# Layer 2's normalizing, turning and first choice moved into the last turns of layer 1

## The reference, cut to what matters

```python
for layer in (0, 1, 2, 3):
    xn = _layernorm(x, axis=-1)
    x = x + attn[layer](xn) + ffn[layer](xn)
```

```python
logits = xt @ Wr + br
probs = jax.nn.softmax(logits, axis=-1)
gate, idx = jnp.max(probs, axis=-1), jnp.argmax(probs, axis=-1)
```

## Time and profile before

| what | value |
|---|---|
| median of three runs | 1791.4 us |
| lowest and highest | 1785.49 and 1794.98 us |
| the profiled execution | 1796.15 us |
| its span, first to last instruction | 1794.3 us |
| busy share of the span: PE, DVE, ACT, POOL | 84%, 64%, 48%, 25% |
| mean granted clock of PE | 0.915 |
| the chain that ended last: PE, DVE, issue, DMA, ACT, POOL | 59%, 15%, 9%, 5%, 4%, 4% |

### The profile page before, as it was taken

The page is one execution under the profiler, slowest core; times in us unless marked ns, Lnnn a source line. Parts: engine busy times, 40 slices in busy tenths (PEclk is TensorE's granted clock), DMA queues, the critical chain, the costliest instruction groups (busy, mean ns, idle before and its releaser), DMA issues.

```text
span 1794.3 us, 41191 instructions
## 1 busy us (share of the span) xinstructions
PE 1502.5 (84%) x11707; PEld 945.8 (53%) x11707; DVE 1149.0 (64%) x3266; ACT 866.6 (48%) x1971; POOL 445.7 (25%) x542
## 2 busy tenths in 40 slices
PE   5356899999998877999997478899999699999998
PEld 4112566656565355888886134455554245555554
DVE  6733566667566865666665556566667667777774
ACT  1022344444444423444442045566665268788887
POOL 3465223223222112222223521122222211000000
PEclk9996799999898858999996589999999779999999
DMA  8431344544543403233320223444442011111110
GB/s 261 127 136 58 102 152 136 175 123 148 160 129 101 116 1 130 107 141 141 129 107 21 97 65 114 135 138 138 138 138 76 21 42 52 53 50 52 47 51 12
DMA packets 127876, 184.77 MB, mean 103 GB/s; under 512 B 14657, under 2 KB 107217, under 8 KB 125345
## 3 DMA queue, kind: packets, MB, share of 16 engines
q1 hardware_dynamic: 94864, 144.54, 25.1%
q10 hardware_dynamic: 26112, 25.17, 4.8%
q0 software_dynamic: 6816, 14.02, 2.2%
HBM read 148.44 MB, written 42.84 MB: 107 GB/s over the span
## 4 chain that ended last, share of the span: by engine, by line
PE 59%; DVE 15%; issue 9%; DMA 5%; ACT 4%; POOL 4%; another core or an unknown queue 1%; SPq 1%; DVEq 1%; ACTq 0%; POOLq 0%
PE pH L528 8%; PE pO L733 7%; PE pT_ L594 6%; PE pY L541 6%; PE pH L620 6%; PE pY L628 5%; DVE mx L1339 3%; PE pS L676 3%; PE pS L698 3%; DMA stk<-packed_qk 2%; ACT pex L847 2%; PE pT_ L592 2%; POOL sorted_x L991 2%; PE pT_ L512 2%; DMA packed_qk<-qk 1%
## 5 line engine op out<-in xcount | busy, mean ns | idle before, releaser
L847 ACT ACTIVATE pex<-pT_ 128x512 f32<-128x512 f32 (+1 forms) x768 | 427.1, 560 | 495.8 <-PE pT_ L594 361.1
L1339 DVE TENSOR_REDUCE mx<-pS 128x2 f32<-128x512 f32 x512 | 347.9, 689 | 154.5 <-PE pS L571 107.5
L594 PE MATMUL pT_<-stk 32*128 32x256 f16 x1024 | 203.9, 285 | 90.9 <-DMA stk<-packed_qk 31.0
L888 POOL DMA_INDIRECT home_y<-ysb,home x117 | 115.1, 984 | 543.4 <-DVE ysb L1362 283.2
L571 PE MATMUL pS<-stk 32*128 32x256 f16 x1024 | 208.3, 291 | 27.6 <-DVEq L1082 17.6
L733 PE MATMUL pO<-pex,va 128*9 128x256 f32 (+1 forms) x3072 | 206.6, 390 | 2.6 <-ACT pex L847 2.6
L594 PEld LDWEIGHTS pT_<-stk 32*128 32x128 f16 x1024 | 55.7, 93 | 209.5 <-issue 86.4
L840 ACT ACTIVATE wb<-pH,b 128x256 f32<-128x256 f32 x256 | 107.3, 470 | 106.6 <-PE pH L528 106.2
L528 PE MATMUL pH<-XT,w 128*128 (+1 forms) x512 | 132.0, 386 | 1.1
L620 PE MATMUL pH<-xsT,wb 128*128 128x128 f32 x888 | 132.4, 294 | 0.3 <-ACT xsT L816 0.3
L851 ACT ACTIVATE pT_<-later 128x384 f32<-128x384 f32 x256 | 126.6, 494 | 8.1
(11 more groups left out here) (220 smaller groups left out, 2584.6 us busy)
## 6 DMA issues: line engine op xcount, KB each, us to landing
wb<-in_w SPq DMA_DIRECT2D x72, 514.0 KB
stk<-packed_qk ACTq DMA_DIRECT2D x96, 256.0 KB, 2.7
wb<-in_w SPq DMA_DIRECT2D x39, 578.0 KB
packed_qk<-qk SPq DMA_DIRECT2D x144, 128.0 KB, 2.0
wb<-gates_turned SPq DMA_DIRECT2D x8, 2048.0 KB, 7.0
pex<-gates_turned SPq DMA_DIRECT2D x8, 2048.0 KB, 7.1
xsb<-sorted_x SPq DMA_DIRECT2D x111, 64.5 KB, 4.1
sorted_x<-in_c_places SPq DMA_DIRECT2D x4, 1548.0 KB, 15.7
```

What stands on the lines that cost most here:

```text
L594: return pe.matmul(bank[:, part * T:(part + 1) * T], key, stk[rows, side, j, 0:T], start=True, stop=True)
L847: ins = act.activation(pex[:, k % 8, 0:n], bank[:, 0:n], ACT.Exp)
L888: pool.indirect_dma_start(YH, bass.IndirectOffsetOnAxis(ap=home[:, place_:place_ + 1], axis=0), ysb[:, place_, :], None).then_inc(sem(f"ho ...
L1339: ins = dve.tensor_reduce(mx[:, :, j, col], bank.rearrange("p (c n) -> p c n", c=2), AX.X, ALU.max)
```

## The change

Seven of layer 2's eight groups leave its prologue. Turn 10 + g of layer 1 now handles group g (tiles 4g to 4g + 3, rows 2g and 2g + 1), for g from 0 to 6: all their rows have been final for some turns. `q` is POOL's inverse deviation (DVE first signals that the statistics are there), `x` DVE's normalizing, `a` the turning (PE, then ACT's copy), `b` the logits (PE, then ACT's copy). Both use bank 1 of `pT_`. In turn 15 the choice for the first half (groups 0 to 3) is made as well, in three pieces `k0` to `k2`. The lists become

```diff
+GROUPS = NT // 4
+AHEAD = {0: 0, 1: 0, 2: 7, 3: 0}
+EARLY = {0: GROUPS, 1: 8, 2: GROUPS, 3: 8}
+AHEAD_FROM = B + 1 - AHEAD[2]
+if AHEAD[2]:
+    CHOICES[B - 1] = (2, 0)
-LOOPS = {0: (2, 12), 1: (2, 14), 2: (2, 14), 3: (2, 14)}
+LOOPS = {0: (2, 12), 1: (2, 10), 2: (2, 14), 3: (2, 14)}
...
+        if AHEAD_FROM <= n:
+            turned, turns = 2 * GROUPS + n - AHEAD_FROM, True
+        chooses = n in CHOICES
+        frame = when(turns, ("q", turned)) + ["F"] + when(behind, ("B", 0)) + when(here, ("Z", 0)) + ["F"] + add(0)
+        frame += when(turns, ("x", turned)) + ["F"] * 2 + when(here and behind, ("e", 0)) + when(chooses, ("k", 0))
+        frame += when(ahead, ("G", 0)) + add(1) + ["F"]
+        frame += when(here, ("N", 0)) + ["F"] + when(turns, ("a", turned)) + ["F"] + add(2) + ["F"]
+        frame += when(chooses, ("k", 1)) + ["F"] + when(ahead, ("R", 0)) + ["F"] + when(turns, ("b", turned)) + ["F"]
+        frame += add(3) + when(chooses, ("k", 2)) + ["F"] + when(here, ("A", 0))
...
+            def turn_late(l, g):
+                pe.wait_ge(sem("xn_ready"), PRIMED + l * GROUPS + g + 1)
+                pe.wait_ge(sem("logits_copied"), PRIMED + l * GROUPS + g)
+                for u in range(4):
+                    ins = pe.transpose(pT_[:, 1, u * P:(u + 1) * P], XN[:, 4 * g + u, 0:P], ident[:, :])
+                ins.then_inc(sem("turned"), 1)
+
+            def logits_late(l, g):
+                pe.wait_ge(sem(f"ld_{l}"), full[f"ld_{l}"])
+                pe.wait_ge(sem("xts_ready"), PRIMED + l * GROUPS + g + 1)
+                for u in range(4):
+                    t = 4 * g + u
+                    ins = pe.matmul(pT_[:, 1, u * 16:u * 16 + EXPERTS[l]], XT[:, t * P:(t + 1) * P], wr[l][:, :],
+                                    start=True, stop=True)
+                ins.then_inc(sem("logits"), 1)
...
+                    elif kind == "a":
+                        g = k % GROUPS
+                        act.wait_ge(sem("turned"), PRIMED + k + 1)
+                        act.activation(XT[:, g * 4 * P:(g + 1) * 4 * P], pT_[:, 1, :], ACT.Copy)\
+                           .then_inc(sem("xts_ready"), 1)
...
+                    elif kind == "q" and k >= 2 * GROUPS and l == 1:
+                        dve.sem_inc(sem("stats"), 1)
+                    elif kind == "x":
+                        normalize(*divmod(k, GROUPS))
+                    elif kind == "k":
+                        of, part = CHOICES[turn.n]
+                        dve.wait_ge(sem(f"ld_{of}"), full[f"ld_{of}"])
+                        choose(of, part, (k,))
...
-                    choose(l, 0)
+                    if not AHEAD[l]:
+                        choose(l, 0)
...
-                    dve.sem_inc(sem("stats"), NT // 4)
+                    dve.sem_inc(sem("stats"), GROUPS - AHEAD[2])
```

More of the change, by code:

```diff
@@ L132, in turn_steps @@
         when = lambda cond, *steps: list(steps) if cond else []
-        frame = ["F"] + when(behind, ("B", 0)) + when(here, ("Z", 0)) + ["F"] * 3 + when(here and behind, ("e", 0))
-        frame += when(ahead, ("G", 0)) + ["F"]
-        frame += when(here, ("N", 0)) + ["F"] * 4 + when(ahead, ("R", 0)) + ["F"] * 3 + when(here, ("A", 0))
+        added, turned = EARLY[1] + n, GROUPS + EARLY[1] + n - 1
+        adds, turns = here and added < GROUPS, here and GROUPS + EARLY[1] <= turned < 2 * GROUPS
+        add = lambda part: when(adds, ("m", 4 * added + 2 + part))
+        if AHEAD_FROM <= n:
[7 more added lines that the diff above has]
+        frame += add(3) + when(chooses, ("k", 2)) + ["F"] + when(here, ("A", 0))
     else:
@@ L852, in take_turn @@
                         ins.then_inc(s("T_free"), 1)
+                    elif kind == "a":
+                        g = k % GROUPS
+                        act.wait_ge(sem("turned"), PRIMED + k + 1)
+                        act.activation(XT[:, g * 4 * P:(g + 1) * 4 * P], pT_[:, 1, :], ACT.Copy)\
+                           .then_inc(sem("xts_ready"), 1)
+                    elif kind == "b":
+                        of, g = divmod(k, GROUPS)
+                        act.wait_ge(sem("logits"), PRIMED + k + 1)
+                        act.activation(LG[:, g * 4:g * 4 + 4, 0:EXPERTS[of]],
+                                       pT_[:, 1, 0:64].rearrange("p (u e) -> p u e", e=16)[:, :, 0:EXPERTS[of]],
+                                       ACT.Copy).then_inc(sem("logits_copied"), 1)
+                    elif kind == "k" and k == 1:
+                        exponents(*CHOICES[turn.n])
                     elif kind == "G":
@@ L899, in _, with inverse_deviation @@
                             .then_inc(sem("w3_ready"), 1)
-                for g in range(NT // 4):
+                def inverse_deviation(l, g):
                     four = slice(4 * g, 4 * g + 4)
@@ L905, in _ @@
                     pool.tensor_tensor(rstd[:, four], vare[:, four], neghalf[:, four], ALU.pow).then_inc(sem("rstd"), 1)
+                for g in range(AHEAD[l], EARLY[l]):
+                    inverse_deviation(l, g)
                 if l == 0:
@@ L963, in take_turn @@
                             send_home(place_)
+                        elif kind == "q":
+                            inverse_deviation(*divmod(k, GROUPS))
+                        elif kind == "k" and k == 2 and CHOICES[turn.n][0] == 1:
+                            pool.wait_ge(sem("gates_late"), 1)
                         elif kind == "Z":
@@ L1047, in choose @@
-                    for t in tiles:
-                        m = chain.mark(dve.max(highest[:, t, :], pr[:, t, 0:n]))
-                    chain.wait(m)
-                    chain.link(dve.memset(highest[:, half, TOPK[l]:8], -1.0))
+                    if 1 in pieces:
+                        chain.link(dve.memset(pr[:, half, n:wide], -1.0))
+                        for t in tiles:
+                            m = chain.mark(dve.max(highest[:, t, :], pr[:, t, 0:n]))
+                        chain.wait(m)
+                        chain.link(dve.memset(highest[:, half, TOPK[l]:8], -1.0))
@@ L1051, in choose @@
+                if 2 not in pieces:
+                    return
+                if l == 1:
                     for t in tiles:
@@ L1331, in take_turn @@
                         if l in SORTED and turn.loop is None:
[L1332 removed]
+                            combine(l, *added[l], combined_at(l, turn.n, k))
                     elif kind == "S":
@@ L1415, in take_turn @@
                         dve.sem_inc(s("z_normal"), 1)
+                    elif kind == "m":
+                        combine(l - 1, *added[l - 1], (k,))
+                    elif kind == "q" and k >= 2 * GROUPS and l == 1:
[6 more added lines that the diff above has]
+                        choose(of, part, (k,))
+                        if k == 2 and of == 1:
+                            dve.sem_inc(sem("gates_late"), 1)
                     elif kind == "A":
@@ L1442, in take_turn @@
                 tc.leave()
+            added = {l: ({}, {}) for l in SORTED}
             for l in range(4):
```

91 lines of the change are left out of this document (51 added, 40 removed).

## The result

The changed kernel takes 1785.54 us (median of 20 runs, 1778.27 to 1795.24), the kernel before 1791.46 us (20 runs, 1778.64 to 1802.08). The ratio is 0.9962, 95% interval 0.9945 to 0.9979: 5.9 us or 0.33% less on the medians, 0.38% by the ratio. Forecast were 1785.0 us and a gain of 0.36%, which the prediction counted as no change, being under 0.5%; with 20 runs each the interval does exclude 1.

What follows compares the result with a forecast made beforehand. PE was taken to bound layer 1's turns and, at half clock, layer 2's prologue. -15.9 saved + 7.7 turns + 0.6 waits + 1.2 stall = -6.4 us, from 1791.4 to 1785.0 us; eight-in-ten range 1778 to 1793.

Steps and rivals of the forecast that it cites:

- What the change saves behind the last turn: From layer 1's last residual add to layer 2's second choice: 14.82, 0.45 and 0.64 us saved, together 15.9 us.
- What it costs in the turns: Layer 1's turns 10 to 15: 1.28 us more PE work each, 7.7 in all, plus 0.6 for waits on normalizing.
- The price from the neighbours in the turn: Added PE passes in layer 1's turns cost 0.107 us each, like nearby instructions there: 12 x 0.107 = 1.28 us a turn.
- the 2.45 us of layer 2's prologue: Upper price of a group in a turn; rival "Moved, not removed" took it: sum +0.6, 1792 us, chance 0.20.
- Turn 15's stall: The choice and normalizing in DVE's queue delay the last hidden gating by 3.5 us, stalling PE's last Y piece 1.2 us.
- the idle time that I let the choice fill: Turn 15, DVE: 1.03 us idle ahead of the last hidden gating and 0.9 inside a pair of gatings absorb added work.
- The 0.9 us inside the pair of gatings: DVE counted as idle for 0.9 us within the pair at 942.62, 2.28 us for two gatings of 0.69.
- Sum: All terms together: -15.9 + 7.7 + 0.6 + 1.2 = -6.4 us, giving 1785.0 us, 0.36% less.
- The clock stays up: Rival: group 6's work in PE's pause before layer 2's prologue holds full clock; 2.15 us more gained, 1782.9 us; chance 0.15.
- The clock falls inside the turns: Rival: short PE work in turns 10 to 15 lowers the clock; slower, 1800 us; chance 0.04.
- Something downstream moves otherwise: Rival: layer 2's start at another instant shifts the return to full clock; 1785 +/- 3 us; chance 0.11.
- last sign: Layer 2: prediction is wrong if the chain from second choice to first heads is not the 41.3 us it was.

Runs made afterwards that it cites:

- a4: `a2` with only four groups moved into turns (13 to 16) and four left in the prologue; ratio 0.995 to the kernel before.
- b1: The kernel before plus unread 512-column matmuls, 24 in PE's pause ahead of layer 2's prologue and two behind each turned group; ratio 0.9933.
- a1: The changed kernel with the third piece of turn 15's choice behind the add of the normalized row; ratio 0.9942 to the kernel before.
- a2: The changed kernel with the first half's choice back in layer 2's prologue; ratio 0.994 to the kernel before.
- d1: The changed kernel itself measured again in a later group, on another chip; 1777.94 us, ratio 0.9915 to the kernel before.
- c2: `c1` plus 17 unread 512-column matmuls in PE's pauses between the last turned output and group 7's logits; ratio 0.9871 to the kernel before.
- d2: The changed kernel with the choice in turn 14 (last piece behind the normalized row's add), `c1`'s move and `c2`'s matmuls; 1770.98 us, ratio 0.9885 to before.
- d5: The kernel before, unchanged, run once more on a fourth chip for a second trace; 43.2 us from second choice to first heads.
- c1: `a2` with group 6's deviation and normalizing moved to the end of turn 15; ratio 0.99 to the kernel before.
- b2: The kernel before with identity transposes, 48 in the pause ahead of layer 2's prologue and four behind each turned group; ratio 0.9977.

## Why the prediction was right, point by point

- *What the change saves behind the last turn*, 15.9 us: measured 16.2. Group 7's turning came 14.94 us earlier (14.82 forecast), then 0.67 less to the projections (0.45; the terms of that step add up to 3.62 us and were entered as 3.7, measured are 3.49) and 0.59 less from there (0.64).
- *What it costs in the turns*, 1.28 us each at full clock and 0.1 for the wait on the normalizing: 6.83 us for turns 10 to 14, 1.37 each (1.26 to 1.47), and 1.27 a group by `a4`. The price from the neighbours in the turn was the right one; the 2.45 us of layer 2's prologue belonged to the lower clock, as `b1` shows with 1.71 for a group and two more matmuls. Layer 0's prologue has the slow period at a shown 1.00, which was rightly not taken as proof of speed: the trace of before has no record of the clock ahead of 122.6 us, and the views show 1.00 where there is none.
- *Turn 15's stall*, 1.2 us: the mechanism was right (`a1` and `a2` remove it), the size was 2.0, by which turn 15 is longer than in `a2`. The term that was mis-sized is the idle time that I let the choice fill, 1.9 us. The last gating ends 15.22 us behind the turn's own add of the turned output (933.89 to 949.11), where it ended 11.14 behind it before: 4.1 us later instead of 3.5. DVE's idle time ahead of the last two gatings was 0.27 and 1.03 us and is now 0.18 and 0.18, so the choice filled 0.9 us of it and not 1.9, and the added instructions took 4.1 + 0.9 = 5.0 us instead of 5.4. The 0.9 us inside the pair of gatings was not idle: DVE is busy for the whole 2.28 us, before and after, and it is the two gatings that last longer than the usual 0.69 us, beside two instructions of POOL:

```profile
942.21 1.15 DVE L1450 TENSOR_TENSOR wb<-wb,pex 128x512 f32<-128x512 f32 x1 [0.26 <-DVE hbs L1484]
943.27 1.21 DVE L1450 TENSOR_TENSOR wb<-wb,pex 128x512 f32<-128x512 f32 x1
942.08 0.72 POOL L1039 TENSOR_TENSOR hbs<-hbs,gam 128x256 f32<-128x256 f32 x1 [4.38 <-DVEq L1487]
942.88 1.06 POOL L1040 TENSOR_TENSOR hbs<-hbs,bet 128x256 f32<-128x256 f32 x1
```

  Each gating ends 0.55 us behind the POOL instruction that it started beside. So it is in both traces throughout layer 1: the gatings of this size that start beside one of the two (30 before, 28 after) take 1.07 to 1.21 us and end 0.54 to 0.55 us behind it, all others 0.66 to 0.73. The remaining 0.2 us of the stall's size lie between the last product's start and the last residual add (2.29 us, from 949.16 to 951.45; 2.07 by the prediction's reckoning of before).
- *Sum*, -6.4: the traces say -6.2, the medians -5.9. The errors nearly cancel: 0.8 us too little for the stall, against 0.3 too little saved, 0.1 too much for turns 10 to 14 and 0.2 by which the turns ahead of them came out shorter. That the medians agree as well is luck: in the series of `d1` the same kernel gained 12.3 us by the medians, where its places say 6.3.
- *The clock stays up*: it did not. In this trace it fell at 951 us, 0.5 us ahead of the last residual add and 2.3 ahead of group 6's turning (953.29), which therefore came too late to hold it; in `d1` it fell in the middle of that turning, and in `a1`, `a2` and `a4` behind it, 4.0 to 4.2 us behind the last residual add, always ahead of group 7's. `c2` holds it with added matmuls, and DVE then hides most of the gain; `d2` shows both removed.
- *The clock falls inside the turns*: refuted, 1.00 in all of them.
- *Something downstream moves otherwise*: the changed kernel's first trace had it, 4.6 us, of which 3.4 lie behind the spread's issue beside the weight loads. Forecast were 53.3 us from the origin to the first heads; 57.7 and 52.7 are measured. By its last sign (41.3 us from the second choice to the heads) the prediction would have been wrong with the first trace; 40.9 in `d1` and 43.2 in `d5` show that this stretch moves by itself, so that as a sign it was too sharp.

That the new kernel's ratio is 0.9962 in one series and 0.9915 in another, with intervals that touch at 0.9945, and that the medians of `c1` differ by 15.8 us where its places say 9.0, stays open. The time outside the changed places is 1524.0 us in one trace of the kernel before and 1496.6 in the other, 1512.2 and 1516.8 in the changed one's: that differs by as much as the effect or more.

## What to carry to other kernels

Price moved work by the engine's clock in both places: the same instructions cost PE 1.3 us in a stream that holds the clock and 2.4 us in a prologue that has lost it, and the gain came from that difference. When a block is moved into an engine's instruction stream, look at what is queued behind it there; 2.4 us of the choice ahead of the last gating cost 2 us there, and 0.6 us when they stood behind it. Before counting on idle time in a merged row, see whether the engine is idle in it, or busy with instructions that last longer. If the gain is smaller than the spread between executions, compare marks inside the traces, which repeat to 0.1 us, rather than whole times.

## What the runs showed of the hardware

- Transposes alone held PE's higher clock level for 5.40 us (`b2`), and over 24 of them it rose from 0.50 to 1.00 (layer 3's prologue, kernel before).
- A weight load of 128 x 128 32-bit values with an 8-column pass takes 0.10 us in the turns at 2.4 GHz (eight in 0.81) and 0.20 in layer 2's prologue at 1.2 GHz (eight in 1.57, from 969.49 to 971.06, before): short passes double in rate with the clock like long ones (the projections take 1.11 and 2.05 us).
- The two parts of a spread of packed rows, issued by one queue 1.15 us or more behind the first of another queue's three loads of 578 KB, go with a start of PE's heads 0.9 to 3.5 us later than where they are issued 1.06 us or less behind it (four traces and eight).
- A 128x512 32-bit `tensor_tensor` of DVE that starts while POOL runs its 128x256 `tensor_tensor` ends 0.54 to 0.55 us behind POOL's (58 of 58), and takes 1.07 to 1.21 us instead of 0.66 to 0.73.
